# Two reciprocals of a threshold search, made on GpSimd as powers instead of on VectorE

## What is computed

```python
def sparsemax(x):
    x = x - jnp.max(x, axis=-1, keepdims=True)
    zs = -jnp.sort(-x, axis=-1)
    rho = jnp.arange(1, L + 1)
    cssv = jnp.cumsum(zs, axis=-1) - 1.0
    k = jnp.maximum(jnp.sum(zs > cssv / rho, axis=-1, keepdims=True), 1)
    tau = jnp.take_along_axis(cssv, k - 1, axis=-1) / k
    return jnp.clip(x - tau, 0.0)

scores = jnp.einsum('bhqd,bhkd->bhqk', qh, kh) * scale      # 512 x 1601 per head
attn = sparsemax(scores)
out = jnp.einsum('bhqk,bhkd->bhqd', attn, vh)
x = x + jnp.tanh(g_xattn[0]) * (out @ Wo + bo)
x = x + jnp.tanh(g_ffn[0]) * moe(layernorm(x))              # 8 experts, top 2
```

## Time and profile before

| | |
|---|---|
| median of 3 runs | 7719.2 us (7714.17 to 7721.12) |
| the profiled execution, its own time | 7722.33 us |
| its span | 7720.4 us |
| attention stage | about 600 to 6550 us of the span |
| busy share of the span | PE 75%, DVE 81%, ACT 76%, POOL 29% |

### The profile page before, as it was taken

How to read it: one execution, slowest core, us unless ns; L and a number is a source line. 1 busy time by engine, 2 the same in 40 slices (tenths; PEclk the granted TensorE clock), 3 DMA queues, 4 the chain that set the end, 5 groups by cost and what they waited for, 6 DMA issues and landing times. The chain is left out here.

```text
span 7720.4 us, 167239 instructions
## 1 busy us (share of the span) xinstructions
PE 5764.2 (75%) x20864; PEld 1911.7 (25%) x20864; DVE 6286.3 (81%) x51708; ACT 5867.6 (76%) x13220; POOL 2216.7 (29%) x10037
## 2 busy tenths in 40 slices
PE   8966777776776776767767777677777776899999
PEld 5531111111111111111111111111111111566666
DVE  5559999999999999999999999999999997444443
ACT  3329889998998998988989999899999997222222
POOL 2213333333333333333333333333333333000000
PEclk9986666666666666666666666666666766899999
DMA  6651111111111111111111111111111111111110
GB/s 210 219 177 23 30 29 28 30 30 28 29 32 29 29 31 27 30 26 29 31 28 30 30 29 32 27 29 29 32 28 31 29 31 37 63 46 49 40 44 22
DMA packets 315602, 344.11 MB, mean 45 GB/s; under 512 B 113912, under 2 KB 238464, under 8 KB 314240
## 3 DMA queue, kind: packets, MB, share of 16 engines
q1 hardware_dynamic: 311936, 324.40, 15.4%
q0 software_dynamic: 2304, 8.39, 0.3%
HBM read 212.38 MB, written 120.10 MB: 43 GB/s over the span
## 5 line engine op out<-in xcount | busy, mean ns | idle before, releaser
L851 DVE MAX8 a_cand<-a_scores 128x8 f32<-128x42 f32 (+1 forms) x38912 | 4367.2, 186 | 213.6 <-issue 210.5
L619 ACT ACTIVATE a_junk_act<-a_cand,a_ntau 128x304 f32<-128x304 f32 (+1 forms) x4096 | 2065.9, 517 | 102.6 <-DVE a_ntau L725 51.3
L584 PE MATMUL a_ring<-a_q,a_k 99*128 99x512 bf16 (+1 forms) x3328 | 1487.4, 560 | 743.4 <-ACT a_scores L643 438.1
L647 ACT ACTIVATE a_attn<-a_ring 128x1024 f32<-128x1024 f32 (+1 forms) x1792 | 1648.9, 969 | 128.8 <-PE a_ring L584 126.4
L643 ACT COPY a_scores<-a_ring 128x1024 f32<-128x1024 f32 (+1 forms) x2048 | 1605.5, 825 | 143.7 <-DVEq L817 74.5
L580 PE MATMUL a_ring<-a_k,a_q 96*128 96x512 bf16 (+1 forms) x4096 | 1324.3, 453 | 404.2 <-ACT a_scores L643 371.0
L534 PE MATMUL a_out<-a_attn,a_v 128*16 128x512 f32 (+1 forms) x6656 | 1545.9, 795 | 1.7 <-ACT a_attn L647 1.7
L580 PEld LDWEIGHTS a_ring<-a_k,a_q 96*128 96x128 bf16 x4096 | 361.3, 115 | 2031.5 <-ACT a_attn L647 980.0
L619 ACT ACTIVATION_READ_ACCUMULATOR a_junk_act<-a_cand,a_ntau 128x1 f32 x4096 | 823.1, 201 | 0.0
L584 PEld LDWEIGHTS a_ring<-a_q,a_k 99*128 99x128 bf16 (+1 forms) x3328 | 306.1, 123 | 1590.2 <-ACT a_scores L643 1215.6
L1187 ACT ACTIVATE e_hid<-e_hid_ps,e_b_in 128x512 f32<-128x512 f32 x256 | 172.9, 686 | 669.8 <-PE e_hid_ps L1134 669.4
(11 more groups left out here) (172 smaller groups left out, 5911.8 us busy)
## 6 DMA issues: line engine op xcount, KB each, us to landing
a_k<-k_parts SPq DMA_DIRECT2D x1536, 50.0 KB
k_parts<-p_ks SPq DMA_DIRECT2D x48, 800.5 KB, 7.4
o_parts<-a_o SPq DMA_DIRECT2D x1024, 32.0 KB, 1.6
e_o<-o_parts SPq DMA_DIRECT2D x64, 512.0 KB, 6.5
p_ctx<-in_ctx_t SPq DMA_DIRECT2D x16, 1601.0 KB, 8.5
v_heads<-p_v SPq DMA_DIRECT2D x16, 1536.0 KB
a_q<-q_parts SPq DMA_DIRECT2D x1536, 16.0 KB
a_v<-v_heads SPq DMA_DIRECT2D x256, 96.0 KB
```

Source lines behind the costliest of these rows:

```text
L584: mm = nc.tensor.matmul(at[0:rows, m * BANK:(m + 1) * BANK], k_st[0:SCORE_ROWS + TAU_ROWS, ut, c * P:c * P + rows], q_st[0:SCORE_ROWS + TA ...
L619: ins = nc.scalar.activation(into[:, t].rearrange("p (a b) -> p a b", a=CHUNKS), cand[:, u % SLOTS, t, :, 0:w], ACT.Relu, bias=ntau[:, u % ...
L647: nc.scalar.activation(attn[0:rows, n, 0:w], at[0:rows, 0:w], ACT.Relu).then_inc(piece_used, 1)
L851: ins = V.max(cand[:, u % SLOTS, t, c], scores[:, u % SLOTS, t, lo:hi])
```

## The change

GpSimd makes both reciprocals itself, as a `TENSOR_TENSOR` with the operation power, whose second operand is a constant 128x4 tile `inverse` filled with -1. The clamp before each reciprocal moves with it. VectorE's L731, L732, L737 and L738, the generator `slope` on VectorE and the semaphores `fall_made` and `inv_made` go away; `counted` now rises with VectorE's last count. One memset is added at the set-up.

```diff
+        inverse = sb("inverse", [P, TILES])
...
-        SETUP = 5 + TILES
+        SETUP = 6 + TILES
...
+            nc.vector.memset(inverse[:], -1.0).then_inc(setup, 1)
...
                     ins = measure_count(t, c[:, t, :, 0:SECOND], CHUNKS * SECOND, nt, count4[:, t:t + 1])
-                yield from link(ins)
-                yield from link(V.tensor_scalar(count4[:], count4[:], 1.0, None, ALU.max))
-                V.reciprocal(per_count[:, u % 2], count4[:]).then_inc(counted, 1)
-
-            def slope(i, u, link):
-
-                dve.wait_ge(fall_made, i + 1)
-                yield from link(V.tensor_scalar(w1[:], fall[:], 1e-30, None, ALU.max))
-                V.reciprocal(per_fall[:], w1[:]).then_inc(inv_made, 1)
+                ins.then_inc(counted, 1)
...
-                    if t == 3 and has(i, 1):
-                        yield from slope(i - 1, prev, link)
...
                     pool.wait_ge(excess_made, ROUNDS * i + 1)
                     pool.sem_inc(passed_pool, 1)
-                    link(G.tensor_scalar(over[:], e, 3.0, -1.0, ALU.min, ALU.add))
+                    G.tensor_scalar(over[:], e, 3.0, -1.0, ALU.min, ALU.add)
+                    link(G.tensor_scalar(count4[:], count4[:], 1.0, None, ALU.max))
+                    link(G.tensor_tensor(per_count[:, u % 2], count4[:], inverse[:], ALU.pow))
                     G.tensor_tensor(newton[:], over[:], per_count[:, u % 2], ALU.mult)
...
                     link(G.tensor_tensor(fall[:], e[:, 1], e[:, 2], ALU.subtract))
-                    G.tensor_tensor(fall[:], fall[:], weight[:], ALU.mult).then_inc(fall_made, 1)
+                    link(G.tensor_tensor(fall[:], fall[:], weight[:], ALU.mult))
                     G.tensor_scalar(over[:], e[:, 2], -1.0, None, ALU.add)
-                    pool.wait_ge(inv_made, i + 1)
-                    pool.sem_inc(passed_pool, 1)
+                    link(G.tensor_scalar(fall[:], fall[:], 1e-30, None, ALU.max))
+                    link(G.tensor_tensor(per_fall[:], fall[:], inverse[:], ALU.pow))
                     link(G.tensor_tensor(inv[:], square[:], per_fall[:], ALU.mult))
```

More of the change, by code:

```diff
@@ L470, in attend_program @@
         excess_made = sem("excess_made")
-        fall_made = sem("fall_made")
-        inv_made = sem("inv_made")
         bad_ready = sem("bad_ready")
@@ L729, in start @@
                     ins = measure_count(t, c[:, t, :, 0:SECOND], CHUNKS * SECOND, nt, count4[:, t:t + 1])
-                yield from link(ins)
-                yield from link(V.tensor_scalar(count4[:], count4[:], 1.0, None, ALU.max))
-                V.reciprocal(per_count[:, u % 2], count4[:]).then_inc(counted, 1)
-            def slope(i, u, link):
-                dve.wait_ge(fall_made, i + 1)
-                yield from link(V.tensor_scalar(w1[:], fall[:], 1e-30, None, ALU.max))
-                V.reciprocal(per_fall[:], w1[:]).then_inc(inv_made, 1)
-            FIRST_LINKS, LAST_LINKS = 2 + 1 + 4 + 2 + 1, 2
+                ins.then_inc(counted, 1)
+            FIRST_LINKS, LAST_LINKS = 2 + 1 + 4, 2
             def links_before(i):
@@ L864, in _ @@
             G = nc.gpsimd
-            FIRST_LINKS, LAST_LINKS = 6 + 4 + 5, 5 + 3
+            FIRST_LINKS, LAST_LINKS = 7 + 4 + 8, 5 + 3
             def links_before(i):
```

## The result

The changed kernel takes 7953.3 us (median, 7950.0 to 7954.6) against 7718.6 us: ratio 1.0304, 95% interval 1.0286 to 1.0322, 234.7 us slower. The forecast was slower by 84 us, 7806. The time lies in the wide range of the forecast, 7700 to 8050, but the loss is 2.8 times the one that was forecast.

The account below looks back on a forecast made before the run. ScalarE was taken to set the pace in most steps. 240 steps at 0.30 + p, p = 0.5, lose 192 us; VectorE's lead gains 108; net 84 on 7722 gives 7806 us, range 7700 to 8050.

Parts of the forecast that it names:

- What bounds the kernel: Attention steps of 22.52 us: ScalarE sets the pace in most, VectorE is held at `fall`, `second` has 0.07 us slack.
- the 14 left out: Of 254 steps running `second`, 14 where the delay disappears in ScalarE's long wait for settling, leaving 240 that pay.
- `second`, 0.35 + p: GpSimd's `second` ends 0.35 + p us later (p: the power's length), so ScalarE's round 1 starts 0.30 + p later.
- The power's length, p = 0.5: Length of one 128x4 power on GpSimd, shown by no row: taken as 0.5 us, with ends 0.2 and 2.13.
- VectorE's lead, 108 us: VectorE, freed of its wait at L737, runs up to 1.75 us earlier; ScalarE's waits on it shrink by 108 us.
- `slope`, nothing below p = 2.4: GpSimd's `slope` ends 0.27 + p us later against 2.64 us of slack before round 3: no cost below p = 2.4.
- VectorE's lead outweighing the power: Rival at ScalarE's waits on VectorE: gain up to 198 us against 120 lost with a short power, 7644 us; chance 0.15.
- The clock: Rival: a new pause shifts TensorE's clock, a third of steps escape ScalarE's waits, 92 us back, 7714 us; chance 0.07.
- The slow power: Rival: GpSimd works the power out element by element, p = 2.13, net loss 475 us, 8197 us; chance 0.12.
- More unsettled tiles: Rival: inexact power worsens the search; 60 more full passes on VectorE add 180 us, 7986 us; chance 0.04.

Follow-up runs that it names:

- doubled power: The full change plus a second, linked power in `second`, written to a spare tile, against the full change: 8250.0 us, 296.7 us above it.
- Slope alone: Kernel before with only the slope's reciprocal moved to GpSimd, `second` as before: 7645.4 us, ratio 0.9910; run again 7640.5 us, ratio 0.9902.
- `second` alone: Kernel before with only the reciprocal of `second` moved to GpSimd, VectorE keeping `slope` and its wait for `fall`: 7983.6 us against 7713.7.

## Why the prediction was right and wrong

**What bounds the kernel**: right. ScalarE set the pace, and GpSimd, idle for two thirds of the time, was on its path at `second`. The doubled power lengthens the median step by 1.19 of its 1.22 us. 240 steps had been counted; the new wait stands in all 254. What was meant by the 14 left out, a delay that disappears in a later wait for VectorE, is real and larger: it comes with the lead, below.

**`second`, 0.35 + p**: right in form. With p = 1.04 the formula gives 1.39 for the chain; measured 4.28 - 2.95 = 1.33. ScalarE's delay, 0.30 + p = 1.34 a step, is 1.29 in the median.

**The power's length, p = 0.5**: this is the term that failed. It is 1.04. The product's row gave 0.0019 us for a simple operation on one more column, and I took 10 to 100 of them for a power and then a value below the middle of what that gave (0.28 to 1.0), "nearer to the row of its own shape". Measured, (1.037 - 0.199) / 4 = 0.21 us for a column, if the fixed part is the product's: 110 simple operations, just outside my bracket. The row of the same shape was near in shape and far in kind. Why a power takes so long, and how much of it is fixed, stays open: every power that ran had this one shape. With the measured p the sum gives 240 x 1.34 - 108 = 214 us, 7936, 17 from the measured time. The error of the net, 151 us, is 240 x 0.54 = 130 from p alone. That the rest is so small is partly luck: the lead was taken some 33 us too large and what a longer step gives back at least 24 too small, and the two nearly cancel.

The Trainium skill's ratio of 1.96 ("GPSIMD Engine Reference", section 3) gave p = 0.30 and missed by more; it was for an addition. Its direction, that elementwise work belongs on VectorE, holds: 1.04 against 0.154 us is a factor of 6.7.

**VectorE's lead, 108 us**: right in mechanism and 1.4 times too large. Slope alone shows it by itself: 75 us. By its parts: for the guess and the tau of `second` 45 were taken and 48.0 - 8.2 = 40 came; for settling and the turned tau 53 were taken and 118.9 - 86.7 = 32 came, perhaps since not every event had the whole 1.75 us of lead, which was not looked at one by one; for the tau of `third` 10 were taken and 1 came. In the changed kernel itself the four rows without the tau of `second` fell by 107.5, where the lead alone takes 64 off them, because the longer step hides VectorE's lateness too. With `second` alone, where VectorE has no lead, the longer step takes 78 us off them (185.0 to 106.6). The prediction had of this only the 14 steps left out, 14 x 1.34 = 19 us. Against it stand 24 us more of ScalarE's waits for TensorE, which the prediction did not have.

**`slope`, nothing below p = 2.4**: right, and shown: with one power there ScalarE has no wait for the tau of `slope` but one of 3.6 us, and a second, which uses the slack up, costs 27 us.

**The rivals.** VectorE's lead outweighing the power did not happen, but it is what the slope alone does. The clock: ScalarE waited for TensorE in more steps than before, not fewer (255 in place of 245, 260 in place of 237), so it went the other way and by little. The granted clock of the attention, between the copies, was 0.66 before and 0.65 after. The slow power lay nearer than thought: 1.04 is between the forecast's 0.5 and the rival's 2.13. More unsettled tiles: the full pass over a tile (L759, now L751) ran 40 times in both kernels, so the search left no more tiles unsettled:

```profile
L759 DVE SCALAR_TENSOR_TENSOR a_junk<-a_scores,a_ntau,a_zeros x40: 1886/1887/1910, 732.8 to 6512.4; 128x1601 f32<-128x1601 f32 x40
```
```profile
L751 DVE SCALAR_TENSOR_TENSOR a_junk<-a_scores,a_ntau,a_zeros x40: 1886/1887/1899, 738.6 to 6748.2; 128x1601 f32<-128x1601 f32 x40
```

## What to carry to other kernels

An engine that is idle for most of the time can still be on the path: look where the last instruction of its chain ends against the start of the one that uses it, and count the slack there, even where no idle time is printed. One change may put the same instruction into two such chains; split it, for here one half alone won 68 to 75 us and the other alone lost 270. And where an operation has no row, ask what kind of work it is before asking what shape it has: keep the value that the kind suggests, and place what needs only early inputs ahead of the wait for the late one.

## What was not expected of the hardware

A power of two 128x4 f32 tiles on GpSimd takes 1.04 us, with almost no spread (1036 to 1049 ns over the 256 of L897), where a product takes 0.20. A second power right behind the first takes 1.01. And a step lengthened on the engine that sets the pace gave back 78 us elsewhere (with `second` alone moved) and 47 more when it was lengthened again, because it also gave the second-busiest engine time to catch up. The price of such a stall is less than its length times its count.
